# One Newton refinement instead of two stages in the inverse of a gated delta rule kernel, 64x64 matmuls made full size, and all four instruction orders written anew

## What is computed

```
q = l2norm(silu(conv(h @ Wq)));  k = l2norm(silu(conv(h @ Wk)));  v = silu(conv(h @ Wv));  z = h @ Wz
g = cumsum(log decay) within a chunk;  decay[i, j] = exp(g[i] - g[j]) for j <= i
A = -strict_lower(beta * (k @ k.T) * decay)
T = inverse(eye - A)                                  # one per chunk and value head
v_new = T @ (beta * v) - (T @ (beta * k * exp(g))) @ state
out   = (q * exp(g)) @ state + lower((q @ k.T) * decay) @ v_new
state = state * exp(g_last) + (k * exp(g_last - g)).T @ v_new
y    += Wout.T @ (norm_w * rmsnorm(out) * silu(z))
```

## Time and profile before

| what | value |
|---|---|
| median of 3 runs | 5349.92 us (5344.38 to 5359.94) |
| span of the profiled execution | 5350.3 us |
| TensorE matmul busy | 4982.9 us, 93% |
| VectorE busy | 4483.8 us, 84% |
| ScalarE busy | 4371.8 us, 82% |
| GpSimd busy | 2064.9 us, 39% |
| attention loop, roughly | from 118 to 5170 us of the span |

### The profile page before, as it was taken

How to read it: one execution, slowest core, us unless ns; L and a number is a source line. 1 busy time by engine, 2 the same in 40 slices (tenths; PEclk the granted TensorE clock), 3 DMA queues, 4 the chain that set the end, 5 groups by cost and what they waited for, 6 DMA issues and landing times. The chain is left out here.

```text
span 5350.3 us, 132947 instructions
## 1 busy us (share of the span) xinstructions
PE 4982.9 (93%) x38788; PEld 3326.6 (62%) x38788; DVE 4483.8 (84%) x9152; ACT 4371.8 (82%) x9744; POOL 2064.9 (39%) x1433
## 2 busy tenths in 40 slices
PE   5899999999999999999999999999999999999978
PEld 3566666666666666666666666666666666666644
DVE  4888888888888888888888888888888888888853
ACT  3788888888888888888888888888888888888842
POOL 2344434344443434444344444434444343444410
PEclk7999999999999999999999999999999999999988
DMA  3222212121121212212121221212122121221112
GB/s 141 75 63 63 75 62 81 60 70 69 62 81 60 79 60 72 71 62 77 60 82 61 65 74 62 81 59 74 65 66 77 60 79 60 72 70 62 64 65 82
DMA packets 185165, 377.26 MB, mean 71 GB/s; under 512 B 86400, under 2 KB 95744, under 8 KB 184960
## 3 DMA queue, kind: packets, MB, share of 16 engines
q1 hardware_dynamic: 185088, 376.46, 21.8%
HBM read 360.13 MB, written 16.25 MB: 70 GB/s over the span
## 5 line engine op out<-in xcount | busy, mean ns | idle before, releaser
L653 PE MATMUL p_proj<-hid,w_in 128*128 128x512 f32 x3072 | 1620.5, 610 | 32.4 <-POOL ident L1163 29.7
L998 DVE SCALAR_TENSOR_TENSOR conv<-pre,taps,conv 128x512 f32<-128x512 f32 x1536 | 1207.8, 793 | 41.9 <-ACT conv L857 37.6
L911 ACT ACTIVATE x_bd<-x_t 64x512 bf16<-64x512 bf16 x1280 | 804.5, 629 | 215.7 <-DVE x_t L1079 198.9
L1205 POOL TENSOR_TENSOR o_sc<-o_sc,neg_half 128x8 f32<-128x8 f32 x128 | 268.6, 2099 | 1622.0 <-DVE o_sc L1135 1622.0
L653 PEld LDWEIGHTS p_proj<-hid,w_in 128*128 128x128 f32 x3072 | 496.6, 192 | 64.5 <-POOL ident L1163 30.0
L838 PE MATMUL p_out<-h_t,w_out 128*128 128x512 f32 x1024 | 501.9, 613 | 0.8 <-DVE h_t L1140 0.8
L1072 DVE TENSOR_TENSOR y_h<-p_lev,y_h 128x512 bf16<-128x512 f32 x640 | 441.3, 690 | 44.2 <-PE p_lev L707 37.9
L1116 DVE TENSOR_TENSOR vw<-p_b,w_c 128x256 f32<-128x256 f32 x384 | 156.9, 409 | 378.8 <-PE p_b L796 378.8
L1079 DVE STREAM_TRANSPOSE x_t<-y_h 128x512 bf16<-128x512 bf16 x640 | 454.6, 710 | 19.3
L1064 DVE TENSOR_TENSOR q_h<-p_lev,consts 128x512 bf16<-128x512 f32 x640 | 438.6, 685 | 37.9 <-PE p_lev L701 33.3
L1172 POOL TENSOR_TENSOR low<-g_row,consts 128x1024 f32<-128x1024 f32 x128 | 302.1, 2360 | 410.1 <-ACT dec L895 409.9
(11 more groups left out here) (210 smaller groups left out, 12168.4 us busy)
## 6 DMA issues: line engine op xcount, KB each, us to landing
w_in<-in_w_in SPq DMA_DIRECT2D x128, 768.0 KB, 6.2
g_row<-rows_scratch SPq DMA_DIRECT2D x128, 512.0 KB, 3.1
hid<-h_scratch SPq DMA_DIRECT2D x128, 512.0 KB, 7.3
e_row<-exp_rows_scratch SPq DMA_DIRECT2D x128, 512.0 KB, 5.1
w_out<-in_w_out SPq DMA_DIRECT2D x128, 256.5 KB, 2.6
x<-in_x SPq DMA_DIRECT2D x8, 512.0 KB, 10.4
h_scratch<-x SPq DMA_DIRECT2D x8, 512.0 KB, 2.6
y_scratch<-y_acc SPq DMA_DIRECT2D x8, 512.0 KB, 5.6
```

The source lines that it names most:

```text
L653: last = pe.matmul(p_proj[tile % 2][:], w_in[p][:, kt, tile * P:(tile + 1) * P], hid[p][:, kt, :], start=(kt == 0), stop=(kt == KT - 1))
L911: last = act.activation(x_bd[block, :, block], x_t[block], ACT.Copy)
L998: dve.scalar_tensor_tensor(conv[:, tile, :], pre[:, tile, j:j + S], taps[p][:, tile, j:j + 1], conv[:, tile, :], ALU.mult, ALU.add).then_i ...
```

## The change

- The refinement is one step now. `D` multiplies `y_dn` by the matrix in three bf16 parts: the upper halves of the float32 words of `ga` (read in place by `top`, every second bf16 element), the upper halves of `a_rest`, and `a_lo`. VectorE's `F` adds the identity and stores the residual `resid` in float32. GpSimd's `RL` makes `r_lo`, what the upper half leaves out. `G` (in the place of `N`) multiplies the residual by `x_dn`, ScalarE's `v` copies that to bf16 (`g_t`), and `W` sums `x_dn`, two products of the residual with `x_dn`, and one with `g_t`. The tasks `AD`, `d`, `n`, `N`, `E`, `e` are gone. New are `AO` on ScalarE (a quarter of the matrix in bf16, for `Q`), `AR` and `RL` on GpSimd.
- `AB` on VectorE now reads the float32 `ga` after `SL` instead of the bf16 `a_d` after `AD`.
- `Q`, `Z` and `XC` are written as full 128-row matmuls on tiles whose unused parts are zero.
- All four order strings are new; one pass of the loop now holds tasks of five steps instead of four.

```diff
-PE_ORDER = ("Z6@1 P9@2 D0@1 XC@1 D1@1 ON0@0 N0@1 ON1@0 P10@2 N1@1 KK0@2 KK1@2 P11@2 E0@1 P0@3 W0@1 E1@1 TR0@1 "
+PE_ORDER = ("P1@3 G0@1 P2@3 W0@1 P3@3 TR0@1 L@2 P4@3 U0@1 M1@2 G1@1 O0@1 KS1@1 P5@3 Y1@2 TR1@1 W1@1 M2@2 U1@1 O1@1 "
...
-POOL_ORDER = ("OP@0 ON@0 PW@2 GL@3 SL@2 SD1@1 QD@2 SD2@1 AL@2")
+POOL_ORDER = ("PW@2 QD@1 RL@1 SL@2 SD1@1 AR@2 AL@2 SD2@1 GL@3 OP@1 ON@1")
...
                 elif name == "Q":
-                        last = pe.matmul(p_lev[HB:P, u * HB:(u + 1) * HB], a_d[0:HB, u, HB:P], y_h[0:HB, u, :],
-                                         start=True, stop=True)
+                        last = pe.matmul(p_lev[:, u * HB:(u + 1) * HB], a_off[:, u, :], y_h[:, u, :], start=True, stop=True)
...
                 elif name == "D":
                     for u in range(n * 4, n * 4 + 4):
-                        pe.matmul(bank(n)[:, u - n * 4, :], a_d[:, u, :], y_dn[:, u, :], start=True, stop=False)
+                        pe.matmul(bank(n)[:, u - n * 4, :], top(ga[p][:, u, 0, :]), y_dn[:, u, :], start=True, stop=False)
+                        pe.matmul(bank(n)[:, u - n * 4, :], top(a_rest[:, u, :]), y_dn[:, u, :], start=False, stop=False)
                         last = pe.matmul(bank(n)[:, u - n * 4, :], a_lo[:, u, :], y_dn[:, u, :], start=False, stop=True)
-                elif name == "N":
-                        last = pe.matmul(bank(n)[:, u - n * 4, :], x_dn[:, u, :], f0[:, u, :], start=True, stop=True)
-                elif name == "E":
-                        last = pe.matmul(bank(n)[:, u - n * 4, :], ga[p][:, u, 0, :], y1[:, u, :], start=True, stop=True)
+                elif name == "G":
+                        last = pe.matmul(bank(n)[:, u - n * 4, :], top(resid[:, u, :]), x_dn[:, u, :], start=True, stop=True)
                 elif name == "W":
-                    t.wait(pe, "e_done", n + 1)
+                    t.wait(pe, "g_done", n + 1)
+                    t.wait(pe, "rlo")
                     for u in range(n * 4, n * 4 + 4):
-                        pe.matmul(bank(n)[:, u - n * 4, :], f0[:, u, :], x_dn[:, u, :], start=False, stop=False)
-                        last = pe.matmul(bank(n)[:, u - n * 4, :], f1[:, u, :], x_dn[:, u, :], start=False,
+                        pe.matmul(bank(n)[:, u - n * 4, :], r_lo[:, u, :], x_dn[:, u, :], start=False, stop=False)
+                        pe.matmul(bank(n)[:, u - n * 4, :], top(resid[:, u, :]), x_dn[:, u, :], start=False, stop=False)
+                        last = pe.matmul(bank(n)[:, u - n * 4, :], top(resid[:, u, :]), g_t[:, u, :], start=False,
...
-                elif name == "AD":
-                    act.activation(a_d[:], ga[p][:, :, 0, :], ACT.Copy).then_inc(s["ad"], 1)
+                elif name == "AO":
+                    act.activation(a_off[0:HB, :, HB:P], ga[p][0:HB, :, 0, HB:P], ACT.Copy).then_inc(s["aoff"], 1)
...
                 elif name == "AB":
-                    t.wait(dve, "ad")
+                    t.wait(dve, "strict")
-                    dve.tensor_copy(a_bd[half(n), :, half(n)], a_d[half(n), :, half(n)]).then_inc(s["abd"], 1)
+                    dve.tensor_copy(a_bd[half(n), :, half(n)], ga[p][half(n), :, 0, half(n)]).then_inc(s["abd"], 1)
...
-                elif name == "n":
-                    dve.scalar_tensor_tensor(quarter(y1, n), quarter(y_dn, n), 2.0, bank(n), ALU.mult, ALU.add)\
+                elif name == "F":
+                    t.wait(dve, "d_mm", n + 1)
+                    dve.tensor_tensor(quarter(resid, n), bank(n), each(const["ident"], 4), ALU.add).then_inc(s["r_done"], 1)
...
+                elif name == "AR":
+                    pool.tensor_tensor(a_rest[:], ga[p][:, :, 0, :], tops(ga[p][:, :, 0, :]), ALU.subtract).then_inc(s["rest"], 1)
                 elif name == "AL":
-                    pool.tensor_tensor(a_lo[:], ga[p][:, :, 0, :], a_d[:], ALU.subtract).then_inc(s["alo"], 1)
+                    pool.tensor_tensor(a_lo[:], a_rest[:], tops(a_rest[:]), ALU.subtract).then_inc(s["alo"], 1)
+                elif name == "RL":
+                    t.wait(pool, "r_done")
+                    pool.tensor_tensor(r_lo[:], resid[:], tops(resid[:]), ALU.subtract).then_inc(s["rlo"], 1)
```

More of the change, by code:

```diff
@@ L33 @@
 PAD = TAPS - 1
-PE_ORDER = ("Z6@1 P9@2 D0@1 XC@1 D1@1 ON0@0 N0@1 ON1@0 P10@2 N1@1 KK0@2 KK1@2 P11@2 E0@1 P0@3 W0@1 E1@1 TR0@1 "
[L35 to L41, removed]
[3 rows of a table removed]
-POOL_ORDER = ("OP@0 ON@0 PW@2 GL@3 SL@2 SD1@1 QD@2 SD2@1 AL@2")
+PE_ORDER = ("P1@3 G0@1 P2@3 W0@1 P3@3 TR0@1 L@2 P4@3 U0@1 M1@2 G1@1 O0@1 KS1@1 P5@3 Y1@2 TR1@1 W1@1 M2@2 U1@1 O1@1 "
+            "KS2@1 VT0@2 Y2@2 VT1@2 TR2@1 M3@2 P6@3 P7@3 U2@1 O2@1 Y3@2 KS3@1 OY0@0 M4@2 TR3@1 QT@3 KT@3 Y4@2 O3@1 "
+            "M5@2 P8@3 OY1@0 Y5@2 P9@3 P10@3 Q6@2 XD@2 P11@3 ON0@1 Z6@2 ON1@1 D0@2 D1@2 XC@2 KK0@3 KK1@3 P0@4")
+ACT_ORDER = ("YC@1 Z0@2 SV0@2 XC@1 Z1@2 v0@1 C0@3 IV0@1 SV1@2 AO@2 VX0@1 C1@3 XB1@2 OT0@1 v1@1 C2@3 OQ0@1 VX1@1 "
+             "XB2@2 IV1@1 OT1@1 VK0@2 VK1@2 OQ1@1 VX2@1 XB3@2 C3@3 OT2@1 OQ2@1 SK@3 SQ@3 XB4@2 VX3@1 QN@3 KT@3 KN@3 "
+             "OT3@1 OQ3@1 XB5@2 GE@3 XD@2")
+DVE_ORDER = ("SM0@2 F0@1 SM1@2 F1@1 SM2@2 SN1@2 SM3@2 SN2@2 GA0@2 GA1@2 GA2@2 GA3@2 T10@2 T11@2 AB1@2 AB0@2 T0@3 "
[3 rows of a table added]
+POOL_ORDER = ("PW@2 QD@1 RL@1 SL@2 SD1@1 AR@2 AL@2 SD2@1 GL@3 OP@1 ON@1")
 def const_columns():
@@ L528, in bank, with top, tops @@
             return p_out[n][:].rearrange("p (a f) -> p a f", f=P)
+        def top(ap):
+            return ap.bitcast(BF)[:, 1::2]
+        def tops(ap):
+            return ap.bitcast(BF)[:, :, 1::2]
         @block.sync
@@ L664, in emit @@
                     t.wait(pe, "q_act")
-                    t.wait(pe, "v_tok_done", back=1)
+                    t.wait_newest(pe, (1, ("v_tok_done", None)), (2, ("inv_done", None)), (2, ("g_done", None)),
+                                      (1, ("ga_done", None)), (2, ("r_done", None)), (3, ("h_done", None)),
+                                      (4, ("y_added", None)), (1, ("q_sq", None)))
                     for c in range(NC):
@@ L725, in emit @@
                     t.wait(pe, "xdn")
-                    pe.sem_inc(passed, 1)
                     for u in range(U):
-                        last = pe.matmul(p_lev[HB:P, u * HB:(u + 1) * HB], x_dn[HB:P, u, HB:P], p_h[HB:P, u, :],
-                                         start=True, stop=True)
+                        last = pe.matmul(p_lev[:, u * HB:(u + 1) * HB], x_dn[:, u, :], p_h[:, u, :], start=True, stop=True)
                     last.then_inc(s["z6_mm"], 1)
@@ L733, in emit @@
                     t.wait(pe, "xdn")
-                    pe.sem_inc(passed, 1)
                     for u in range(U):
-                        last = pe.matmul(p_tr[0:HB, u * HB:(u + 1) * HB], y_dn[HB:P, u, 0:HB], ident_h[HB:P, HB:P],
-                                         start=True, stop=True)
+                        last = pe.matmul(p_tr[:, u * HB:(u + 1) * HB], y_dn[:, u, :], ident_h[:, HB:P], start=True, stop=True)
                     last.then_inc(s["xt7"], 1)
@@ L765, in emit @@
                     if n == 0:
[L766 to L774 removed]
+                        t.wait_newest(pe, (0, ("g_done", 1)), (-1, ("ga_done", 2)), (0, ("r_done", 1)),
+                                          (1, ("h_done", 1)), (-1, ("k_tok_done", None), ("k_sq", None)),
+                                          (2, ("y_added", 1)), (0, ("v_tok_done", 1)), (1, ("inv_done", 1)))
+                    else:
+                        t.wait_newest(pe, (0, ("g_done", None)), (-1, ("ga_done", None)), (0, ("r_done", None)),
+                                          (1, ("h_done", None)), (2, ("y_added", None)), (-1, ("q_sq", None)),
+                                          (0, ("v_tok_done", None)), (1, ("inv_done", None)))
@@ L920, in emit @@
                     t.wait(act, "d_mm", back=1)
-                    t.wait(act, "n_done", back=1)
                     act.activation(y_dn[HB:P, :, 0:HB], p_lev[HB:P, :].rearrange("p (u f) -> p u f", f=HB), ACT.Copy)\
@@ L1046, in emit @@
                         t.wait(dve, "o_mm", back=2)
-                        t.wait(dve, "e_mm", back=2)
+                        t.wait(dve, "d_mm", back=2)
                     for h in range(HD):
@@ L1154, in _ @@
                 pool.sem_inc(counted, SPARE * counts[name])
-            for tile in (a_bd, x_bd, y_dn):
+            for tile in (a_bd, a_off, x_bd, y_dn, p_h):
                 pool.memset(tile[:], 0.0)
```

112 lines of the change are left out of this document (63 added, 49 removed), and 6 rows, old and new, of the table DVE_ORDER.

## The result

The changed kernel takes 5398.1 us (median; 5395.7 to 5400.7) against 5350.2 us of the kernel before in the same comparison: a ratio of 1.009, 95% interval 1.0076 to 1.0104. It is slower by 48 us, where 5095 us were forecast.

A forecast was written before the change was run, and what follows sets the result against it. TensorE was taken to bound the loop at 39.1 us a step; minus 1.38 of work and 0.6 of waits gave 37.1, so 5350 - 253 = 5097, stated as 5095 us, range 5030 to 5200 (0.60).

The forecast's parts named there:

- TensorE's terms: TensorE per step: `E` -1.88, sixteen added bf16 matmuls +0.92, `Q`, `Z`, `XC` made full -0.42; sum -1.38 us, busy 35.8.
- The strided weight loads: 40 weight loads a step in `D`, `G`, `W` reading every second bf16 element: 0 to +2.4 us, taken as nothing.
- The second rival: Strided weight loads on TensorE are not hidden: up to +2.4 us a step, 5404 us, or 5251 at half; chance 0.13.
- the 0.029 us slot: TensorE's full 64-column matmuls come every 0.029 us with a packed load each, so a doubled load hides behind 0.057 us.
- The 107 ns of the prediction: Skill's price for a slow 128-column weight load; without the fast load, 2.0 us a step more, 5353 us.
- ScalarE and GpSimd: Busy per step: ScalarE falls from 33.5 to 31.8 us; GpSimd rises from 16.0 to 20.3 with `AR` and `RL`.
- VectorE: 34.1 + 0.5 = 34.6: VectorE's busy us per step: `F` for `n` adds 0 to +0.12, `AB` reading float32 adds about +0.4.
- the third rival: GpSimd and VectorE lock each other out, one meeting costing 0.6 to 1.9 us: 5609 us in one case; chance 0.12.
- its point of decision at 1.98 us a step: The lock between VectorE and GpSimd decides when added meetings on the waiting path exceed 1.98 us a step.
- its price for three short meetings, 5379 us: Three short VectorE-GpSimd meetings on the waiting path, 2.2 us a step, put on top of 5097 us.
- The signs that I had named for this rival: VectorE's tap mean above 850 ns or copies above 0.5 us; forecast wrong if TensorE idles past 4 us a step.
- The wait at the bank: TensorE's `N` waits 1.46 us a step for VectorE's `HT` to empty `ON`'s bank; 0.6 of it gained by reordering.

The follow-up runs named there:

- three_meetings_gone: Changed kernel with GpSimd's `ON` also waiting for the copies into `y_dn`, `q_dec` moved behind `low`, and VectorE's `F1` behind `neg_c`: 5037.0 us, ratio 0.941.
- on_after_copies: Changed kernel with GpSimd's `ON` also waiting for VectorE's two copies into `y_dn`: 5233.8 us, ratio 0.9779.

## Why the prediction was wrong

- **TensorE's terms held.** `E` gone, sixteen more bf16 matmuls, three stages made full: busy 35.8 us a step, as worked out. The full stages run at the pace that I took from the 64-column rows: `Z` starts at 3016.57 and the next group at 3016.80. The strided weight loads, for which I had no row, are free. The 24 matmuls of `D` in the changed kernel's timeline, first, last, and the next group:

```profile
3018.38 0.22 PE L765 MATMUL p_out<-y_dn,ga 128*128 128x128 bf16 x1 [0.94 <-DVE h_t L1161]
3018.43 0.22 PE L766 MATMUL p_out<-y_dn,a_rest 128*128 128x128 bf16 x1
...
3019.66 0.22 PE L767 MATMUL p_out<-y_dn,a_lo 128*128 128x128 bf16 x1
3019.72 0.40 PE L750 MATMUL p_tr<-ident_h,y_dn 128*128 128x64 bf16 x8
```

```profile
3016.57 0.39 PE L744 MATMUL p_lev<-p_h,x_dn 128*128 128x64 bf16 x8
3016.80 0.63 PE L852 MATMUL p_out<-consts,o_tok 128*128 128x128 f32 x4
```

  1.34 us for 24, 0.056 each, two of three with a strided load. The second rival (0.13) is out, and the choice by the 0.029 us slot was right. The 81 ns of the Trainium skill, "TensorE: Matmul & The Clock Gate", section "Back-to-back issue gap", do not hold here either, at 0.056 us. My sentence that no pair in the trace of the kernel before is that slow is true of the stretch only: from 172.11 us on, eight matmuls of `D` are 0.106 us apart, at a granted clock of 0.58 (171.2 to 174.0). The 107 ns of the prediction stand, in the same page of the Trainium skill, one section ahead of the one that I named, in "LDWEIGHTS (loading the stationary operand)".
- **ScalarE and GpSimd held**, at 31.7 and 19.6 us. `AR`, `RL` and `AL` take 1.89 to 1.91 us each, less than the 2.14 of the earlier trace rows.
- **The step that failed is VectorE's**, "VectorE: 34.1 + 0.5 = 34.6", and with it the sentence on the third rival that puts one meeting, "the copies meet `ON`, for about 1 us", into the width of the forecast. The edits themselves cost what I said or less: `F` 0.66, the casts 0.42 against the 0.48 that I had put in. The sum of 34.6 holds nothing for any meeting. Three were added, at 3.2 us of VectorE's time a step: copies and `ON` 1.30, `neg_n` and `q_dec` 1.02, `neg_c` and `r_lo` 0.87. A fourth, taps and select, took the place of the old one of taps and `ON` and costs little more, 12 x (808 - 792) ns = 0.19 us. The three cost 164, 101 and 89 us of time, each measured alone; the one that I had foreseen cost all of its 1.28 us a step, not half of 1. The rival had its point of decision at 1.98 us a step, and 361 / 128 = 2.8 us of time came. Its mechanism was right and its chance, 0.12, far too low. That its price for three short meetings, 5379 us, is near the 5398 measured is in part luck: it starts from 5097, where the kernel without them takes 5037, and puts 2.2 us on them instead of 2.8.
- **Why I missed two of them.** I asked only for the big VectorE instructions (taps, copies) beside GpSimd's new order. `q_dec` stands right behind `root`, and so does the small instruction `neg_n` that turns `root` into a scale: they are released by the same event, so they meet every time. `r_lo` is released by the second residual, `F1`, and `neg_c` starts 0.11 us behind the end of `F1` (3021.47 and 3021.58): a close race, which `neg_c` lost in about every other step. An 8-element instruction costs next to nothing alone (0.16 us) and seemed to need no cover; held, it costs what is left of its neighbour. The signs that I had named for this rival were only half of it: the copies (0.94 us, over the 0.5 named) told, while the taps' mean (808 ns, under the 850) and TensorE's idle time (3.7 us, under the 4) did not.
- **The wait at the bank** was as foreseen, moved and shortened: `D0` waits for `HT` for 57.4 us in the stretch, 0.94 us a step instead of 1.46. The gain of 0.6 that I gave it would have come: `three_meetings_gone` idles TensorE for only 0.9 us a step in all, against my 1.3, and `D0` no longer waits for `HT` there but, for 0.3 us a step, for ScalarE.

The Trainium skill, "GPSIMD Engine Reference", section "Key points", says that GpSimd shares its SBUF interfaces with VectorE, with contention for VectorE instructions in a two-port mode or with two SBUF inputs. The trace agrees on who is held. The taps and `neg_c` have two SBUF inputs. The copies and `neg_n` have one source in SBUF and a target there, for which the Trainium skill, "VectorE: DVE Perf Modes", section "What auto-detection actually checks", names the mode 2×_2P; that they run in it is not shown by any run. The trace also agrees on who is not held: the casts out of PSUM (`p_h`, L1110) take 694 ns in `on_after_copies`, where they run beside `ON`, and 695 in the kernel before (one from 2999.45, `ON` from 2998.92 to 3000.82). How long an instruction is held is read from the rows above: until the GpSimd instruction has ended.

## What to carry to other kernels

Work moved to an engine with free time is not free if its instructions hold up those of the engine that bounds the step: lay the two engines' orders side by side at every place where one event releases both, and count the small instructions there too. A mean duration that does not fit an instruction's size is the sign of it in a profile, and if the mean lies between the free and the fully held duration, compare single steps. A wait added on the other engine can be worth more than the work saved (164 us for one line here). Before removing a meeting, ask whether the held time lies beside a wait anyway: two of the edits here removed held time and lost 28 and 79 us.

## What the runs showed of the hardware that was not expected

- A tap, a copy, `neg_n` or `neg_c` on VectorE and a long instruction on GpSimd exclude each other by whole instructions; the one that starts second stands, in both directions, and even with 8 elements. `neg_n` and `neg_c` went from 0.16 us to 1.24 us behind `q_dec`, 1.89 behind `r_lo` and 2.19 behind `low`. GpSimd's select, with one input, takes part: it went from 1098 to 1444 ns beside a tap and held the next tap.
- Not every GpSimd instruction holds VectorE. `OP`, a power over 8 elements, takes 1.65 us (3010.24 to 3011.89 in the changed kernel), and the tap that starts inside it, at 3011.36, takes its usual 0.74 us.
- Reading the upper halves of float32 words as weights costs nothing: 0.056 us a matmul, as with packed ones.
- A saving of 0.28 us a step on the bounding engine made a kernel 3.6% slower, by turning round the order of two instructions on two other engines; one wait brought it to 0.2% faster. The meeting came in about every other step: there `low` started 0.18 us ahead of `neg_c`, and one step later 0.11 us behind it (3066.21 and 3066.32). Why the two kinds of step differ was not tried.
- The best version that ran is `three_meetings_gone`: 5037 us, 5.9% faster than the kernel before and 6.7% faster than the changed one.
